# Attention on one core: scores first into the PSUM bank, mask products added on top

## The reference, cut to what matters

```
L0 cross attention   s = q.k/sqrt(8), keys hidden where the mask is 0
L1 attention         s = q.k/sqrt(8) + relative position bias, causal
L2 attention         s = q.k/sqrt(8), causal (4 key heads shared by 16)
L2 block's attention s = q.k/sqrt(8), causal
L3 attention         y  = softmax(s, causal) v          (v = x)
                     y2 = softmax(s2, causal) (v shifted - y)    a second pass over 8 batches
a = softmax(s);  out = a v;  x = x + out Wo
```

## Time and profile before

| | us |
|---|---|
| median of 3 runs | 1256.82 |
| lowest, highest | 1253.72, 1261.24 |
| the profiled execution's own time | 1258.97 |
| its span | 1257.3 |

### The profile page before, as it was taken

One profiled execution on the slowest core, in us unless ns is written; L12 is line 12 of the kernel. 1 busy time (PEld: TensorE's weight loads), 2 busy tenths in 40 slices (PEclk: granted clock), 3 DMA queues, 4 the chain that ended last, 5 costly groups with the idle time before them and its releaser, 6 DMA issues. The chain is left out here.

```text
span 1257.3 us, 30097 instructions
## 1 busy us (share of the span) xinstructions
PE 1019.8 (81%) x12232; PEld 712.5 (57%) x12232; DVE 845.9 (67%) x1508; ACT 535.0 (43%) x1334; POOL 563.9 (45%) x390
## 2 busy tenths in 40 slices
PE   7557888887889989998293998898696999857795
PEld 2246766666674555555282456555495555533795
DVE  6689999999986776567343786587323688755243
ACT  5634444444433642552141572274152777502121
POOL 3389999999965512101455200211433321003232
PEclk9759999999998999999596998899798999978898
DMA  3668888888863000000482000000573000003692
GB/s 117 147 185 226 234 226 234 230 229 229 221 247 133 2 1 1 2 1 1 131 247 82 1 2 1 1 2 1 196 244 112 1 1 2 1 1 134 239 305 78
DMA packets 74904, 139.82 MB, mean 111 GB/s; under 512 B 8544, under 2 KB 28912, under 8 KB 74544
## 3 DMA queue, kind: packets, MB, share of 16 engines
q1 hardware_dynamic: 70800, 129.72, 35.4%
q0 software_dynamic: 3968, 8.18, 1.8%
HBM read 128.04 MB, written 14.82 MB: 114 GB/s over the span
## 5 line engine op out<-in xcount | busy, mean ns | idle before, releaser
L897 ACT ACTIVATE shifted_a<-scores,nmax_a 128x128 f32<-128x128 f32 x768 | 208.1, 388 | 79.3 <-DVE nmax_a L841 77.7
L1542 ACT ACTIVATE decay<-decay 128x1016 f32<-128x1016 f32 x128 | 123.9, 1002 | 150.9 <-PE decay L1427 150.9
L841 DVE TENSOR_REDUCE nmax_a<-scores 128x4 f32<-128x512 f32 x192 | 123.5, 685 | 70.2 <-PE scores L727 68.1
L373 POOL TENSOR_TENSOR rstd<-ve,neghalf 128x4 f32<-128x4 f32 x30 | 31.5, 1050 | 252.8 <-DVE ve L358 252.8
L1427 PE MATMUL decay<-delta,A_pairs 32*128 32x127 f32 x2048 | 82.7, 302 | 74.5 <-DVE small_pack L1586 33.9
L847 DVE COPY PTs_a<-PT 128x512 f32<-128x512 f32 x192 | 122.9, 680 | 2.8 <-PE PT L737 2.8
L1427 PEld LDWEIGHTS decay<-delta,A_pairs 32*128 32x128 f32 x2048 | 69.6, 203 | 93.2 <-DVE small_pack L1586 38.6
L1884 POOL DMA_INDIRECT results<-xs_s x76 | 72.8, 958 | 104.3 <-DVE xs_s L2059 96.7
L737 PE MATMUL PT<-mamba_pack,shifted_a 128*128 128x128 f32 x768 | 106.5, 280 | 4.4 <-DVE PTs_a L847 2.6
L737 PEld LDWEIGHTS PT<-mamba_pack,shifted_a 128*128 128x128 f32 x768 | 82.7, 141 | 30.6 <-issue 19.3
L1094 POOL TENSOR_TENSOR pos_bias<-pos_bias,B 128x1024 f32<-128x1024 f32 x37 | 89.3, 2453 | 5.0 <-POOLq L1106 2.6
(11 more groups left out here) (483 smaller groups left out, 2296.4 us busy)
## 6 DMA issues: line engine op xcount, KB each, us to landing
pos_bias<-du_rows SPq DMA_DIRECT2D x74, 256.0 KB, 4.9
small_pack<-L3f_w SPq DMA_DIRECT2D x15, 768.0 KB, 5.5
O<-du_rows SPq DMA_DIRECT2D x38, 256.0 KB, 4.6
masked_cos<-du_rows SPq DMA_DIRECT2D x36, 256.0 KB, 4.8
masked_sin<-du_rows SPq DMA_DIRECT2D x36, 256.0 KB, 5.0
XN<-du_rows SPq DMA_DIRECT2D x36, 256.0 KB, 4.8
XNT<-du_rows SPq DMA_DIRECT2D x36, 256.0 KB, 4.7
small_pack<-L2f_w SPq DMA_DIRECT2D x15, 514.0 KB, 5.1
```

Of the source, the lines that this page charges most:

```text
L373: nc.gpsimd.tensor_tensor(rstd[:, bs], ve[:, bs], m.neghalf[:, bs], ALU.pow).then_inc(m.rstd_ready, 1)
L841: nc.vector.tensor_reduce(nmax[:, u % 4, :], scores[u % 4], AX.X, ALU.min).then_inc(m.maxed, 1)
L897: t = nc.scalar.activation(shifted[u % 4][:, j, :], scores[u % 4][:, j, :], ACT.Exp, scale=-1.0, bias=nmax[:, u % 4, j:j + 1])
L1542: nc.scalar.activation(x, x, ACT.Exp, scale=-1.0).then_inc(decayed, 1)
```

## The change: what it does

In each pair of units the scores are written first and open the accumulation (start=True); the products of the masks follow, add on top, and the last of them increments `scored`. The waits for the bank move with the first writer, from `add_bias` to `score`. In the loop a pass issues `turn(u), turn(u+1)`; the late projection or `turn_back`; `score(u+4), score(u+5), add_bias(u+4), add_bias(u+5)`; `weigh(u-2), weigh(u-1)`. In the turned calls the late projection of the queries now stands ahead of the first units.

```diff
             def add_bias(u):
+                parts = (bias if u < B * NG else second.bias)(u % NG, u // NG % B)
+                for k, (w, x) in enumerate(parts):
+                    t = nc.tensor.matmul(scores[u % 4], w, x, start=False, stop=(k == len(parts) - 1))
+                t.then_inc(m.scored, 1)
+
+            def score(u):
+                g, b = u % NG, u // NG
+                rows = slice(32 * g, 32 * g + 32)
                 if u >= 4:
                     pe.wait_ge(m.exped, U0 + u - 3)
                 elif u >= 2 and inputs is not None:
@@
-                for k, (w, x) in enumerate((bias if u < B * NG else second.bias)(u % NG, u // NG % B)):
-                    nc.tensor.matmul(scores[u % 4], w, x, start=(k == 0), stop=False)
-
-            def score(u):
-                g, b = u % NG, u // NG
-                rows = slice(32 * g, 32 * g + 32)
                 if g == 0:
                     pe.wait_ge(m.kh_ready, B0 + b + 1)
@@
-                nc.tensor.matmul(scores[u % 4], QT[rows, ...], KH[b % 2][rows, :, :], start=False,
-                                 stop=True).then_inc(m.scored, 1)
+                nc.tensor.matmul(scores[u % 4], QT[rows, ...], KH[b % 2][rows, :, :], start=True,
+                                 stop=False)
@@
-            for u in (0, 1):
-                add_bias(u)
             if turned:
                 inputs.product(pe, 0, 1)
-            for u in (0, 1):
-                score(u)
-            for u in (2, 3):
-                add_bias(u)
-            for u in (2, 3):
-                score(u)
+            for first in (0, 2):
+                for u in (first, first + 1):
+                    score(u)
+                for u in (first, first + 1):
+                    add_bias(u)
@@
                 turn(u)
                 turn(u + 1)
-                if u + 4 < UNITS:
-                    add_bias(u + 4)
-                    add_bias(u + 5)
@@
                 if u + 4 < UNITS:
                     score(u + 4)
                     score(u + 5)
+                    add_bias(u + 4)
+                    add_bias(u + 5)
```

More of the change, by code:

```diff
@@ L726, in score @@
                         inputs.wait_ready(pe, 0, b // 4)
-                nc.tensor.matmul(scores[u % 4], QT[rows, b % B * S:(b % B + 1) * S], KH[b % 2][rows, :, :], start=False,
-                                 stop=True).then_inc(m.scored, 1)
+                nc.tensor.matmul(scores[u % 4], QT[rows, b % B * S:(b % B + 1) * S], KH[b % 2][rows, :, :], start=True,
+                                 stop=False)
             def turn(u):
```

## The result

The changed kernel takes 1260.76 us (median of 20 runs, 1255.08 to 1265.53), the kernel before 1254.58 us (20 runs, 1248.90 to 1261.24). The ratio of the two, with its 95% interval, is 1.0046 [1.0030, 1.0062]: 5.8 us slower, 3.8 to 7.8 (the medians alone differ by 6.2). The forecast was +4.4 us.

A forecast was written before the change was run, and what follows sets the result against it. TensorE's sequence of products, busy throughout the loops, was taken as the bound. The terms 7.0 - 0.9 - 0.4 - 0.05 - 1.3 = +4.35, rounded +4.4 us, took the median from 1256.82 to 1261.2 us, range 1257 to 1266.

The forecast's parts named there:

- What bounds: In the attention loops TensorE never stops, 46.28 of 46.28 us busy in L3, so its sequence of products bounds them.
- The loop term: Full-size-mask calls: one more change of array shape in each of 68 loop passes, 0.103 us each, +7.0 us.
- the L0 loop: Six L0 passes with `turn_back` each become 0.15 us shorter, the others stay the same: -0.9 us.
- the pass u = 0: First loop pass of each call: an exposed weight load goes, in L0 a change of shape too; -0.2 and -0.2 us.
- the ends: Ends of the calls: the last pair's first scores complete earlier, shortening TensorE's wait; 4 x 0.2 and 0.5 in L1, -1.3 us.
- The estimate by the drain of 128 cycles: Alternative price for the extra loop changes of shape: 0.053 us a drain, 4 us in place of 7.
- The starts: Starts of the calls: L1 +0.2, L2 block +0.1, L3 +0.25, L2 -0.2, L0 -0.4, together -0.05 us.
- `turn_back` and `PO`: Moved `turn_back` finds ScalarE's `PO` copy ready with 0.04 us to spare, cost 0; rival that it waits: +3.8, chance 0.12.
- the clock rival: L0 loses its 6.9 us half-clock stretch, 3.4 us saved, or another call's start gains one, +3.4; chance 0.10 together.

The follow-up runs named there:

- e1: The changed kernel's loop, with the first four units of each call mask products first as before the change; 1.0056 of the kernel before, +7.0 us.
- e2: The kernel before, with scores first only for the first four units of each call; 0.9996 of the kernel before, -0.5 us.
- e4: The changed kernel with the loop's mask products moved behind `weigh`, three changes of shape a pass; 0.9979 of the kernel before, -2.6 us.
- e5: The kernel before, with `weigh(u-2)` moved between the pair's two mask blocks, two more changes of shape a loop pass; 1.0200 of the kernel before, +25 us.
- e7: The kernel before, with the L0 mask product on 128 rows (64 of them zeros) in place of 64; 0.9972 of the kernel before, -3.5 us.

## Why the prediction was right

**What bounds.** Right: TensorE's order. Seven periods with 46.28 of 46.28 busy became seven with 47.76 of 47.76, and the forecast was 47.7.

**The loop term, 68 x 0.103 = +7.0.** Right: the fourteen passes above are longer by 47.76 - 46.28 = 1.48, so 0.106 each, and 68 of them 7.2. It is shown from four sides: with the changed loop alone the kernel loses (e1), with the starts alone it doesn't (e2), the scores first with three changes of shape take 3.04 a pass (e4), two changes more and no product more cost +25 us (e5). That the whole of e1 measured +7.0, like this one term, is chance: e1 also holds the L0 loop, the pass u = 0 and the ends, and is +5.0 by call.

The estimate by the drain of 128 cycles, which the Trainium skill gives on the page TensorE: Matmul & The Clock Gate, Step-by-step, was 4 us for this term; the trace has 0.093 us a change, not 0.053. The Trainium skill has it on the page TensorEngine Tiling (Array Packing), Key Properties, that changing the tiling mode drains the engine. The traces agree so far as a pause stands at each such place, and e7 shows that 64 x 128 to 128 x 128 counts as a change too; that the pause is a drain they don't show.

**The L0 loop, -0.9.** Right: passes with `turn_back` take 3.63 in place of 3.78, the others 3.19 as before.

**The starts, -0.05.** Right in sum and in each full-mask call, as the calls of e2 show.

**The ends, -1.3.** Right: the wait ahead of the transposes of unit 30 fell by 0.52 in L1 and by 0.21 in the others.

**`turn_back` and `PO`.** Right, by a hair. ScalarE's copy and the weight load behind it, changed kernel:

```profile
1006.27 0.60 ACT L903 ACTIVATE POs_a<-PO 128x512 f32<-128x512 f32 x1 [0.98 <-PE PO L758]
...
1006.95 0.47 PEld L771 LDWEIGHTS back<-mamba_pack,POs_a 128*128 128x128 f32 x4
```

1006.87 and the handover of 0.05 make 1006.92, and the load goes at 1006.95, where it would go anyway. No pass pays.

**What it missed: +0.3 in L3.** In the pass u = 8 TensorE turns rows for the second half (L625), behind a wait for `normalise` (`out_done`), VectorE's division by the row sums. The prediction counted the waits of `turn_back` and left this one out, though the bias that used to stand ahead of it moved away as well. TensorE and VectorE there, changed kernel:

```profile
995.28 1.09 PE L739 MATMUL PT<-mamba_pack,shifted_a 128*128 128x128 f32 x8
996.50 0.71 PE L625 MATMUL back<-mamba_pack,XNT 128*127 128x128 f32 x4
...
996.15 0.29 DVE L852 TENSOR_TENSOR O<-back,rsum_a 128x128 f32<-128x128 f32 x1
```

Transposes to `turn_rows` (the rows of L625) are 1.22 in place of 0.93: 0.29 of waiting until 996.15 + 0.29 = 996.44. The pass took 3.70 before and takes 4.03, +0.33 in place of +0.10. That is 0.23 of the 0.3; the rest is that a pass costs 0.106 and not 0.103, 29 times. In e4, where the scores of the pass before are complete later still, the pass u = 8 takes 4.60.

**The size.** +4.4 forecast, +4.7 in the traces at clock 1.0, +5.8 (3.8 to 7.8) in the runs: the same within what the runs can tell. The forecast was made for L0 with its half clock in both kernels. In the first pair of profiles the changed kernel lost that stretch, as the clock rival had it, and 3.45 us with it; how often either kernel has one was not counted, so its share in the 5.8 us stays open.

## What to carry to other kernels

Where TensorE is the bound, price its order by distances from start to start and count the changes of array shape in one pass of the loop: here one more cost 0.10 us a pass, weight load included, and a product placed between two of its own shape is free of them. When a block moves, list every wait that it used to stand in front of, the rare passes too. Compare calls, not spans: outside the attention calls two executions of the changed kernel differed by 5.1 us, and in each of them by at most 0.01.

## What the runs showed of the hardware

The pause is the same 0.09 us from 128 x 128 to 32 x 128 (bias to scores 0.52 for two products, 0.43 without it) and to 128 x 32 (0.53 against 0.44 for four transposes), and with 64 x 128 on either side (e7 saves 0.10 and 0.26 a pass). Out of 32 x 128 it is part of the 1.06 of the scores, the same to bias and to `weigh`, and out of 128 x 32 part of `weigh`, 0.36 to bias and to transposes in e5; there it can't be told from the weight loads. It is invisible in busy shares and idle columns (46.28 us busy of 46.28, and 47.76 of 47.76). Two products with a mask of 128 rows, zeros in 64 of them, took 0.53 with the change of shape behind them, like two of 64 rows, and saved the change ahead of them. The granted clock fell to 0.50 for 6.9 us at the start of L0 in one execution of the kernel before and for 3.4 us in another, and not at all there in e5, which has the same order of instructions up to that place.
